# Splitting one more tile of D in the late odd groups, and giving one low part of C to VectorE

## The reference

```python
def _cin(x, weights, biases):          # x: (512, 32, 64)
    hidden = x
    for i, (w, b) in enumerate(zip(weights, biases)):
        z = einsum('bhd,bfd->bhfd', hidden, x).reshape(B, hidden.shape[1] * 32, 64)
        y = relu(einsum('bcd,oc->bod', z, w) + b[None, :, None])
        if i != n_layers - 1:
            hidden, direct = (y[:, :64, :], y[:, 64:, :])
        else:
            direct = y
        finals.append(direct)
    return concatenate(finals, axis=1).sum(-1)
h = relu(concatenate([z, dense_ctx], 1) @ W_top1 + b_top1)
h = relu(h @ W_top2 + b_top2)
y = h @ W_top3
```

## Time and profile before

| what | value |
|---|---|
| median of 3 runs | 1042.33 us |
| lowest and highest | 1041.72 and 1042.46 us |
| the profiled execution | 1041.68 us |
| its span from first to last instruction | 1039.9 us |
| granted TensorE clock, mean | 0.989 |
| busy: PE, DVE, ACT, POOL | 96%, 90%, 77%, 91% |

### The profile page before, as it was taken

How to read it: one execution, slowest core, us unless ns; L and a number is a source line. 1 busy time by engine, 2 the same in 40 slices (tenths; PEclk the granted TensorE clock), 3 DMA queues, 4 the chain that set the end, 5 groups by cost and what they waited for, 6 DMA issues and landing times.

```text
span 1039.9 us, 11650 instructions
## 1 busy us (share of the span) xinstructions
PE 999.7 (96%) x3586; PEld 673.9 (65%) x3586; DVE 938.8 (90%) x807; ACT 799.8 (77%) x967; POOL 944.9 (91%) x325
## 2 busy tenths in 40 slices
PE   2399999999999999999999999999999999999999
PEld 1146666666667666676667676767676767676763
DVE  3089999999999999999999999999999999999981
ACT  6057777778888888888888888888888888888872
POOL 6619999999999999999999999999999999999980
PEclk9599999999999999999999999999999999999999
DMA  6498877777878877777787788778867676767620
GB/s 175 86 241 194 196 190 190 184 184 192 198 185 197 187 193 182 191 189 188 188 201 185 178 197 193 186 181 194 193 167 180 167 187 172 174 177 190 164 67 0
DMA packets 140832, 184.20 MB, mean 177 GB/s; under 512 B 55697, under 2 KB 56337, under 8 KB 140642
## 3 DMA queue, kind: packets, MB, share of 16 engines
q1 hardware_dynamic: 136178, 179.19, 70.7%
q0 software_dynamic: 4096, 4.20, 1.8%
q10 hardware_dynamic: 496, 0.06, 0.0%
HBM read 174.92 MB, written 8.39 MB: 176 GB/s over the span
## 4 chain that ended last, share of the span: by engine, by line
PE 88%; POOL 7%; issue 2%; SPq 1%; DMA 1%; ACT 1%; POOLq 0%; DVE 0%; ACTq 0%
PE py L837 30%; PE py L860 16%; PE py L846 15%; PE py L847 15%; POOL zl L433 3%; POOL emb L422 3%; PE py L869 2%; PE py L875 2%; PE py L868 2%; PE py L889 1%; DMA xs<-x_dram 1%; POOLq L150 0%; PE pzB L949 0%; PE py L849 0%; PE pzS L949 0%
## 5 line engine op out<-in xcount | busy, mean ns | idle before, releaser
L433 POOL TENSOR_TENSOR zl<-zf,zh 128x1536 fp32r<-128x1536 f32 (+1 forms) x183 | 799.3, 4391 | 29.0 <-ACT zh L509 27.3
L723 DVE TENSOR_TENSOR zf<-xs,hid 128x2048 f32<-128x2048 f32 (+1 forms) x256 | 536.8, 2106 | 28.0 <-ACT hid L546 23.7
L509 ACT ACTIVATE zh<-zf 128x2048 fp32r<-128x2048 f32 x189 | 345.9, 1830 | 94.3 <-DVE zf L723 91.1
L837 PE MATMUL py<-zf,wf 128*128 128x512 f32 x800 | 364.2, 592 | 1.6 <-DVE zf L723 1.6
L846 PE MATMUL py<-zh,wh 128*128 128x512 f32 x751 | 292.9, 390 | 0.0
L847 PE MATMUL py<-zh,wl 128*128 128x512 f32 x751 | 292.3, 389 | 0.0
L837 PEld LDWEIGHTS py<-zf,wf 128*128 128x128 f32 x800 | 150.9, 189 | 143.8 <-issue 130.0
L860 PE MATMUL py<-zl,wh 128*128 128x512 f32 x751 | 230.7, 428 | 0.8 <-POOL zl L433 0.8
L860 PEld LDWEIGHTS py<-zl,wh 128*128 128x128 f32 x751 | 140.8, 188 | 60.7 <-issue 32.5
L846 PEld LDWEIGHTS py<-zh,wh 128*128 128x128 f32 x751 | 141.0, 188 | 30.4 <-issue 0.2
L847 PEld LDWEIGHTS py<-zh,wl 128*128 128x128 f32 x751 | 141.0, 188 | 29.9 <-issue 0.2
(11 more groups left out here) (116 smaller groups left out, 702.6 us busy)
## 6 DMA issues: line engine op xcount, KB each, us to landing
xs<-x_dram SPq DMA_DIRECT2D x512, 256.0 KB
xs<-x_dram SPq DMA_DIRECT2D x252, 64.0 KB
xt_pair<-x_dram SPq DMA_DIRECT2D x128, 64.0 KB
x_pair<-x_dram SPq DMA_DIRECT2D x128, 64.0 KB
x_dram<-emb SPq DMA_DIRECT2D x66, 64.0 KB
x_dram<-emb SPq DMA_DIRECT2D x22, 96.0 KB
emb<-in_tbl,idx POOLq DMA_INDIRECT x128
x_dram<-emb SPq DMA_DIRECT2D x4, 384.0 KB
```

Of the source, the lines that this page charges most:

```text
L433: pool.tensor_tensor(zl[:, q, first:end], zf[:, s, first:end], zh[:, q, first:end].bitcast(F32), ALU.subtract).then_inc(lo["P"], 1)
L509: act.activation(zh[:, q, first:end], zf[:, s, first:end], ACT.Copy).then_inc(hi, 1)
L723: dve.tensor_tensor(zf[:, slot(u), first:T], left[:, first:T], view(right, at, [[0, T - first], [1, N]]), ALU.mult).then_inc(mult, 1)
L837: mm = pe.matmul(y, wf[:, w, h], zf[:, s, h], start=first and h == first_tile, stop=ends and h == T - 1)
```

## The change

In the ten odd groups from 43 to 61, D's tile 2 is split as its tile 3 was: `main` leaves both out of the whole matmuls, `high_e` and `low_e` each take two tiles (1024 columns) in one instruction, and `split_e` has six matmuls where it had three. In the same groups the low part of C's tile 0 is taken from GpSimd's instruction, which then has 1536 columns where it had 2048, and VectorE makes it in an instruction of its own (`low_first`), behind products B and ahead of `sum_2`. A semaphore `first_lo` tells TensorE and the next user of the buffer.

```diff
+def first_by_vector(unit):
+    name, g = unit
+    return name == "C" and last_split(("D", g))
+
+def low_begin(unit):
+    return 1 if through_bank(unit) or first_by_vector(unit) else 0
...
+        zhE, zlE, whE, wlE = zhB[:, 2:4], zlB[:, 2:4], whB[:, 2:4], wlB[:, 2:4]
...
             def low(u):                                   # GpSimd
-                first, end = 1 if through_bank(u) else 0, split_end(u)
+                first, end = low_begin(u), split_end(u)
                 pool.tensor_tensor(zl[:, q, first:end], zf[:, s, first:end], zh[:, q, first:end].bitcast(F32), ALU.subtract).then_inc(lo["P"], 1)
             def low_e(g):
                     pool.wait_ge(e_hi, NTH_E[g])
-                    pool.tensor_tensor(zlB[:, 2], zf[:, slot(("D", g)), 3], zhB[:, 2].bitcast(F32), ALU.subtract).then_inc(e_lo, 1)
+                    pool.tensor_tensor(zlE, zf[:, slot(("D", g)), 2:T], zhE.bitcast(F32), ALU.subtract).then_inc(e_lo, 1)
...
-                    act.activation(zhB[:, 2], zf[:, slot(("D", g)), 3], ACT.Copy).then_inc(e_hi, 1)
+                    act.activation(zhE, zf[:, slot(("D", g)), 2:T], ACT.Copy).then_inc(e_hi, 1)
...
                         need_low(dve, prev)
+                    if first_by_vector(prev):
+                        dve.wait_ge(first_lo, NTH_FIRST[prev])
...
+            def low_first(u):
+                if first_by_vector(u):
+                    s, q = slot(u), split_slot(u)
+                    dve.wait_ge(hi, NTH_SPLIT[u])
+                    dve.tensor_tensor(zl[:, q, 0], zf[:, s, 0], zh[:, q, 0].bitcast(F32), ALU.subtract).then_inc(first_lo, 1)
...
                 products(("B", g))
                 low_bank(("C", g))
+                low_first(("C", g))
                 if g >= 1:
                     sum_2(g - 1)
...
-                    for h in range(first_tile, T - 1 if last_split(u) else T):
+                    for h in range(first_tile, 2 if last_split(u) else T):
...
                 need_low(pe, u)                           # late
+                if first_by_vector(u):
+                    pe.wait_ge(first_lo, NTH_FIRST[u])
...
                 if last_split(("D", g)):                  # split_e
                     pe.wait_ge(e_hi, NTH_E[g])
-                    pe.matmul(bank(("D", g)), whB[:, 2], zhB[:, 2], start=False, stop=False)
-                    pe.matmul(bank(("D", g)), wlB[:, 2], zhB[:, 2], start=False, stop=False)
+                    for h in range(2):
+                        pe.matmul(bank(("D", g)), whE[:, h], zhE[:, h], start=False, stop=False)
+                        pe.matmul(bank(("D", g)), wlE[:, h], zhE[:, h], start=False, stop=False)
                     pe.wait_ge(e_lo, NTH_E[g])
-                    pe.matmul(bank(("D", g)), whB[:, 2], zlB[:, 2], start=False, stop=False).then_inc(used_e, 1)
+                    for h in range(2):
+                        mm = pe.matmul(bank(("D", g)), whE[:, h], zlE[:, h], start=False, stop=False)
+                    mm.then_inc(used_e, 1)
```

More of the change, by code:

```diff
@@ L109 @@
 NTH_E = {u[1]: i + 1 for i, u in enumerate(v for v in UNITS if last_split(v))}
+NTH_FIRST = {u: i + 1 for i, u in enumerate(v for v in UNITS if first_by_vector(v))}
 NTH_LAST_WHOLE = {u: i + 1 for i, u in enumerate(v for v in UNITS if last_whole(v))}
@@ L179, in dlrm_tower @@
         zl = sb("zl", [P, ZS, T, N], F32R)
-        zhB = sb("zhB", [P, len(OWN), N], F32R)
-        zlB = sb("zlB", [P, len(OWN), N], F32R)
+        zhB = sb("zhB", [P, 4, N], F32R)
+        zlB = sb("zlB", [P, 4, N], F32R)
         zS = sb("zS", [P, N], F32R)
@@ L197, in dlrm_tower @@
         wf = sb("wf", [P, len(WHOLE_NAMES), T, P])
-        whB = sb("whB", [P, len(OWN), P], F32R)
-        wlB = sb("wlB", [P, len(OWN), P], F32R)
+        whB = sb("whB", [P, 4, P], F32R)
+        wlB = sb("wlB", [P, 4, P], F32R)
         wS = sb("wS", [P, 2, P], F32R)
+        zhE, zlE, whE, wlE = zhB[:, 2:4], zlB[:, 2:4], whB[:, 2:4], wlB[:, 2:4]
         xd = [xs[:, 0:T], xs[:, T:2 * T]]
@@ L257, in dlrm_tower @@
         e_hi, e_lo, used_e = sem("e_hi"), sem("e_lo"), sem("used_e")
+        first_lo = sem("first_lo")
         lo = dict(V=sem("lo_v"), P=sem("lo_p"))
@@ L486, in _ @@
                 if name == "D":
-                    act.activation(whB[:, 2], banks[b][:, 3 * P:4 * P], ACT.Copy).then_inc(w_high, 1)
+                    act.activation(whE.rearrange("p t n -> p (t n)"), banks[b][:, 2 * P:4 * P], ACT.Copy).then_inc(w_high, 1)
             act.wait_ge(w_turned, 6)
@@ L670, in _ @@
                 if name == "D":
-                    dve.tensor_tensor(wlB[:, 2], banks[b][:, 3 * P:4 * P], whB[:, 2].bitcast(F32), ALU.subtract).then_inc(w_low, 1)
+                    dve.tensor_tensor(wlE.rearrange("p t n -> p (t n)"), banks[b][:, 2 * P:4 * P],
+                                      whE.rearrange("p t n -> p (t n)").bitcast(F32), ALU.subtract).then_inc(w_low, 1)
                 if name in SPLIT_NAMES:
```

## The result

The changed kernel takes 1053.55 us (median of 6 runs, 1052.95 to 1059.85) against 1042.3 for the kernel before: a ratio of 1.012, 95% interval 1.0106 to 1.0133. It is 11.2 us slower; the forecast was 3.0 us slower, and the range ended at 1050. The profiled execution took 1059.85, the slowest of the six; five lie between 1052.95 and 1053.84.

What follows compares the result with a forecast made beforehand. TensorE sets the pace. The loop lengthens 1.51 against slack 1.17, making the period 29.90 (+0.16); the last low of D starts 1.9 later and is 1.08 longer: +3.0 us, 1045.3 from the median of 1042.33; range 1040.4 to 1050.

Steps and rivals of the forecast that it cites:

- TensorE's work: Each odd group loses a whole tile (0.86) and gains three float32r matmuls (0.68): -0.18 us, ten times that -1.8 us.
- the low of C: GpSimd's low part of C, three tiles for four: 4.61 becomes 3.53 us, -1.08, gained ahead of a wait for ScalarE.
- The loop: TensorE's tail, ScalarE, GpSimd's low of D, late matmuls: lengthening 1.51, slack 1.17, stall 0.34, period 29.90, 0.16 more.
- the ends: First group 0.10 earlier; the kernel's end hangs on group 61's low of D: +1.9 and +1.08 for its length, +3.0 us.
- The rival in which TensorE keeps its pace: The loop grows by less than 1.17 us, so the period falls by 0.18: 1040.7 to 1041.9 us; chance 0.16.
- One reading behind the loop: TensorE, waiting for GpSimd's low part, loads weights meanwhile and goes on in effect 0.05 us ahead of its end.
- VectorE's low part: C's tile 0 on VectorE: waits 0.8 us for GpSimd's low of A, takes 1.4 to 1.5, costs the period nothing.
- the third rival of the prediction: VectorE is shut out by every subtraction until GpSimd idles: period 37.3, +7.6, some +76 in all, 1118 us; chance 0.05.

Runs made afterwards that it cites:

- `d_only`: The changed kernel with only the split of D's tiles 2 and 3; GpSimd makes C's low part whole again: 1045.32 us, ratio 1.0036.
- `turn_given`: The changed kernel plus a wait: GpSimd's low part of C, in the ten groups, waits until VectorE has made its tile 0: 1045.09 us, ratio 1.0033.
- `low_later_59`: The changed kernel with VectorE's turn ordered by a wait, D's low matmuls three matmuls later, and neither part in group 61: 1040.25 us, ratio 0.9987.
- `pause43`: The changed kernel plus one wait: in group 43 GpSimd's low of A waits until VectorE has made products C: 1045.6 us, ratio 1.0039.
- `gather_each`: The changed kernel plus one more GpSimd gather, into an unread buffer, ahead of its low of A in each of the ten groups: 1129.46 us, ratio 1.084.
- `lock_sweep`: Separate kernel without the reference's computation: 102 episodes, one VectorE subtraction against three of GpSimd, arrival varied; let in behind the first in all 97 that met it.
- `from45`: The changed kernel with both parts from group 45 on in place of 43: three runs at 1045.93 to 1046.27 us, three at 1052.88 to 1053.26.
- `lf_after_sum`: The changed kernel with VectorE's new instruction behind `sum_2` instead of ahead of it: 1080.25 us, ratio 1.0357.

## Why the prediction was wrong

**TensorE's work, L541, L453, the low of C: right.** 1.04 and 2.41 us measured for 1.05 and 2.38. The low of C shows 3.96 to 4.01 in the eight groups where VectorE had its turn ahead of it (some 0.45 of that turn is in the record), and 3.53 and 3.56 in the two where it hadn't; 3.53 and a turn of 0.55 were foretold. The mean of 3606 ns above is over all 47 instructions of that shape, 37 of them in earlier groups.

**The loop and the ends: right, and priced a little low.** The period is 29.96 for 29.90, and TensorE's ten waits at the low parts are 0.5 us each for 0.34. `d_only`, which has only this, loses 3.7 us, and `turn_given`, the whole change with the turn ordered, 3.4, for 3.0 foretold; `low_later_59`, which opens the loop and leaves the last group out, takes the loss away and a little more. That the gain on GpSimd lies ahead of a wait and the cost behind it was the point of the forecast, and it holds. The rival in which TensorE keeps its pace is out.

One reading behind the loop was worded wrongly. The prediction says that weights are loaded during the wait; but in the earlier trace rows the load itself waits: L860's starts at 1011.34, 0.06 behind GpSimd's end at 1011.28. L913's in the changed kernel starts 0.05 behind the end of L453 at 764.18:

```profile
764.23 0.30 PEld L913 LDWEIGHTS py<-zlB,whB 128*128 128x128 f32 x2 [0.48 <-POOL zlB L453]
764.57 0.88 PEld L887 LDWEIGHTS py<-zl,wh 128*128 128x128 f32 x4
```

The loads then follow each other faster than at the usual 0.23, so that L887's comes as if TensorE had gone on at 764.57 - 2 x 0.23 = 764.11, 0.06 ahead of the end of L453. The number that the sum used, 0.05 ahead, was right.

**VectorE's low part: the step that failed.** It said that VectorE waits 0.8 us, does its tile at the seam behind the low of A, and costs the period nothing. In eight of the ten groups of the profile this was so: 0.95 to 1.51 us, with 0.4 to 1.0 of waiting, and the next instructions in time. In groups 43 and 57 the third rival of the prediction holds instead, in which VectorE is shut out until GpSimd idles; I had taken it as something for all ten groups or none and gave it 0.05. So what the sum put at nothing costs 7.3 us for each lost turn: once in group 43, and now and then in another group. The rival's price per group was right, 37.28 measured for 37.3. One lost turn and the 3.4 us of `turn_given` make 10.7 of the 11.2 us of the median; the profiled execution lost two turns. `pause43` gives back 8 us by a pause of GpSimd, `turn_given` 8.5 us by an ordered turn, and in `gather_each` every turn is lost. So for group 43, and with it for nearly all of the median's excess over the forecast, the cause is shown: a gather issued by GpSimd, with no idle moment between it and the seam. For group 57, the second turn of the profiled execution, it isn't.

The working had what was needed to doubt. The subtraction at 126.63 in the earlier trace rows stands behind a gather too (at 125.66, 0.96 long). There VectorE was let in, but ahead of another gather, where GpSimd has a gap of 0.16 us; of the seam between two subtractions I wrote that no row shows it, and then priced it as open.

The Trainium skill ("SBUF — State Buffer", "SBUF: two separate sides" and "Who interferes with whom") has the lock go to whichever of the two starts first, and issue order decide who blocks. It doesn't say who goes first at a seam with GpSimd's next subtraction already queued. Read so that VectorE, which has waited longer, goes first there, it agrees with 97 episodes of `lock_sweep`. Behind a gather, with no idle moment since, that reading doesn't hold, nor does issue order decide: VectorE was passed over by up to ten subtractions that started after it had asked.

**Open.** Turns are lost without a gather too: one of 54 such turns in the six runs of the changed kernel and three of 54 in the six of `from45`, counted by their times (one of each is seen in a profile, in groups 57 and 51), and two groups in the profile of `lf_after_sum`. The kernels that measure the turn alone never showed one in 259 episodes without a gather or with a pause behind it, with SyncE's loads or without. What makes them I don't know. Nor does a run here show what it is that a gather leaves behind and an idle moment ends.

## What to carry to other kernels

When work is moved between two engines of a loop, ask on which side of their wait the gain and the cost fall: equal sums can still lengthen it. An instruction of VectorE with two SBUF operands beside a busy GpSimd should get its turn by a semaphore, or be placed where GpSimd idles, and not be priced by its shape. Look at each distinct case of an instruction (the first after a change of phase, here) and not at its median: two of ten made 14.6 of the 17.6 us that the profiled execution lost against the median of the kernel before.

## What the runs showed of the hardware

A subtraction of VectorE (512 columns, two SBUF operands) that meets GpSimd's subtractions is let in at the next seam, 97 of 97 times where nothing else ran, and ends 0.55 us behind the subtraction that it waited for. In the full kernels a few such turns are lost even so. After an indirect DMA issued by GpSimd it isn't let in at any seam between the subtractions that follow (54 of 54 episodes, and ten of ten groups of `gather_each`), for 47.5 us in the longest run tried, until GpSimd has been idle; an idle time of 0.79 us was enough in the kernel. Where GpSimd's next instruction was another indirect DMA, VectorE was let in ahead of it, and that DMA then took 2.83 us where its like takes 0.95. Loads issued by SyncE meanwhile made no difference.
